# A graph layer on one core: a product padded to 128 rows, x + beta spread over two engines, and another order in the first and last steps

## The reference

```python
h = jnp.maximum(_layernorm(x), 0.0)
edge_input = concatenate([h[src], h[dst], edge_attr_32, node_vec[src], node_vec[dst]])
messages = silu(edge_input @ mW1 + mb1) @ mW2 + mb2
aggregated = segment_sum(messages, dst, 50000)
u = silu(concatenate([h, aggregated, node_vec]) @ uW1 + ub1)
out = x + _layernorm(h + u @ uW2 + ub2) * ln_gamma + ln_beta
```

## Time and profile before

| | |
|---|---|
| median of 3 runs (lowest, highest) | 649.43 us (648.74, 649.60) |
| span of the profiled execution | 645.0 us |
| median less that span | 4.4 us |
| busy: PE, DVE, ACT, POOL | 609.0, 594.8, 541.5, 400.7 us |
| TensorE clock granted, mean | 0.987 of full speed |

### The profile page before, as it was taken

The page is one execution under the profiler, slowest core; times in us unless marked ns, Lnnn a source line. Parts: engine busy times, 40 slices in busy tenths (PEclk is TensorE's granted clock), DMA queues, the critical chain, the costliest instruction groups (busy, mean ns, idle before and its releaser), DMA issues.

```text
span 645.0 us, 16065 instructions
## 1 busy us (share of the span) xinstructions
PE 609.0 (94%) x3716; PEld 451.9 (70%) x3764; DVE 594.8 (92%) x2050; ACT 541.5 (84%) x1181; POOL 400.7 (62%) x397
## 2 busy tenths in 40 slices
PE   2888999999999999999999999999999999999972
PEld 1346777776776786786786777777777777777762
DVE  4646899999999999999999999999999999999787
ACT  1578999989989989989989999999999899899730
POOL 6777667567567667667667766766676756761000
PEclk9998999999999999999999999999999999999987
DMA  5645567677677577677587577677676676674432
GB/s 149 200 127 135 145 211 216 165 214 216 165 215 218 171 212 211 170 215 217 163 214 216 169 217 205 173 215 203 178 227 186 179 229 183 201 203 125 134 86 102
DMA packets 92206, 119.02 MB, mean 185 GB/s; under 512 B 20250, under 2 KB 65749, under 8 KB 92168
## 3 DMA queue, kind: packets, MB, share of 16 engines
q1 hardware_dynamic: 64868, 44.03, 25.4%
q10 hardware_dynamic: 14756, 48.66, 20.9%
q0 software_dynamic: 12544, 25.92, 18.9%
HBM read 79.63 MB, written 38.70 MB: 183 GB/s over the span
## 4 chain that ended last, share of the span: by engine, by line
PE 87%; DVE 4%; issue 2%; ACT 2%; POOL 2%; DMA 2%; SPq 0%; POOLq 0%; DVEq 0%; ACTq 0%
PE ps_hid L594 13%; PE ps_upd L606 13%; PE ps_hid L591 12%; PE ps_e L551 8%; PE ps_e L521 8%; PE ps_t L562 7%; PE ps_t L539 6%; PE ps_e L517 6%; PE ps_e L518 6%; PE ps_upd L608 6%; POOL ends_in L456 2%; PE ps_f L529 1%; DVE y_out L894 1%; ACT ends_norm L668 1%; DVE centred L864 1%
## 5 line engine op out<-in xcount | busy, mean ns | idle before, releaser
L456 POOL DMA_INDIRECT ends_in<-in_rows,end_idx x392 | 399.6, 1019 | 182.0 <-issue 167.1
L668 ACT ACTIVATE ends_norm<-ends_in,minus,rstd 128x128 f32<-128x128 f32 x392 | 160.0, 482 | 1.9 <-DVE minus L1008 1.9
L668 ACT ACTIVATE x_norm<-x_in,minus,rstd 128x128 f32<-128x128 f32 x392 | 155.5, 482 | 0.0
L594 PEld LDWEIGHTS ps_hid<-match,msg_in 113*128 113x128 f32 x784 | 102.6, 191 | 47.6 <-issue 37.1
L894 DVE SCALAR_TENSOR_TENSOR y_out<-centred,rstd,x_beta 128x128 f32<-128x128 f32 x392 | 115.4, 338 | 0.2
L606 PE MATMUL ps_upd<-w_out,hidden_n 128*128 128x128 f32 x784 | 105.0, 277 | 2.7 <-DVE centred L864 2.5
L864 DVE SCALAR_TENSOR_TENSOR centred<-ps_upd,stats,gamma_row 128x128 f32<-128x128 f32 x392 | 106.5, 339 | 0.0
L594 PE MATMUL ps_hid<-match,msg_in 113*128 113x128 f32 x784 | 103.6, 275 | 0.0
L591 PE MATMUL ps_hid<-h_t,w_node 128*128 128x512 f32 x196 | 100.4, 593 | 0.0
L606 PEld LDWEIGHTS ps_upd<-w_out,hidden_n 128*128 128x128 f32 x784 | 96.4, 194 | 3.3 <-DVE centred L864 3.3
L766 ACT ACTIVATE hidden_n<-ps_hid,node_bias 128x512 f32<-128x512 f32 x98 | 66.7, 681 | 32.5 <-PE ps_hid L594 32.5
(11 more groups left out here) (81 smaller groups left out, 653.6 us busy)
## 6 DMA issues: line engine op xcount, KB each, us to landing
out<-y_out ACTq DMA_DIRECT2D x48, 512.0 KB
x_in<-in_x_steps ACTq DMA_DIRECT2D x44, 512.0 KB
msg_in<-msgs SPq DMA_DIRECT2D x392, 56.4 KB
msgs<-msg SPq DMA_DIRECT2D x49, 258.0 KB
ends_in<-in_rows,end_idx POOLq DMA_INDIRECT x392
feat_t<-in_attr SPq DMA_DIRECT2D x25, 128.0 KB, 3.3
x_in<-in_x_steps SPq DMA_DIRECT2D x5, 512.0 KB
feat_t<-coords SPq DMA_DIRECT2D x98, 2.0 KB
```

Source lines behind the costliest of these rows:

```text
L456: nc.gpsimd.indirect_dma_start(out=dst, out_offset=None, in_=rows, in_offset=bass.IndirectOffsetOnAxis(ap=end_idx[s.slot // 2][:, s.slot % ...
L594: last = nc.tensor.matmul(ps_hid[:, cols(j)], msg_in[k.half][0:WINDOW + 1, j, 0:H], match[k.half][0:WINDOW + 1, j, :], start=False, stop=j ...
L668: return nc.scalar.activation(dst, source, function, bias=minus[was][:, c:c + 1], scale=rstd[was][:, c:c + 1])
```

## The change

It has these parts:

- The product of the edge features takes 128 rows: w_feat and feat_t are 128 partitions high, and the 94 rows beyond the 34 are cleared by DVE once, at the start.
- x + beta: of the eight tiles of a step, two (POOL_TILES) are summed by POOL, one iteration later than DVE's own, behind its gathers and behind a wait for the match of the step before. DVE sums the other six in two pieces of three, one behind root_r, one behind rstd. The load of x_in and y_out wait for POOL's sums too (x_beta_begun). The first two steps (FIRST_NODES) stay with DVE alone.
- centred has two buffers.
- First iterations: DVE makes the x statistics and x + beta ahead of its wait for the gathers. In iteration 3 PE turns x ahead of the ends, into ps_upd (turns_first); ACT copies h_t ahead of ends_t. ACT's three early norms are left behind hidden_e in the first full iteration. `keep_busy` has two products fewer and writes ps_hid.
- Last iterations: DVE makes the update's statistics between the two matches, and y_out and x + beta behind the roots. ACT stores at the end of its body. For the last three node steps (N_APART; of the very last, its second half) ACT multiplies centred by rstd into y_out (scale_centred), and DVE only adds x_beta, four tiles in one instruction.

```diff
+FIRST_NODES = 2
+POOL_TILES = 2
+N_APART = 3
...
+    def turns_first(self):
+        return self.mode == WHOLE and isinstance(self.n, int) and self.n == NODE_LAG - 1
+    def late(self):
+        return bool(self.node(-1)) and not self.edge(0) and not self.node(4)
+    def scaled_apart(self):
+        done = self.node(-2)
+        if not done or not isinstance(done.n, int) or done.n < NODE_STEPS - N_APART:
+            return range(0)
+        return range(N_TILES // 2 if done.n == NODE_STEPS - 1 else 0, N_TILES)
...
-        w_src, w_dst, w_feat = sb("w_src", [P, H]), sb("w_dst", [P, H]), sb("w_feat", [FEAT, H])
+        w_src, w_dst, w_feat = sb("w_src", [P, H]), sb("w_dst", [P, H]), sb("w_feat", [P, H])
-        feat_t = [sb(f"feat_t{b}", [FEAT, 2, E_STEP]) for b in range(RING // 2)]
+        feat_t = [sb(f"feat_t{b}", [P, 2, E_STEP]) for b in range(RING // 2)]
...
 POOL, body
+                prev, near = it.node(-1), it.node(1)
+                if prev and near:
+                    wait_apart(pool, x_loaded[near.slot], 16 * (near.fills4 + 1), pool_passed)
+                    wait_apart(pool, out_ready, near.n - RING + 1, pool_passed)
...
+                    wait_apart(pool, match_ready, 2 * prev.n + 2, pool_passed)
+                    nc.gpsimd.tensor_tensor(x_beta[near.slot][:, 0:POOL_TILES, :], x_in[near.slot][:, 0:POOL_TILES, :],
+                                            beta_row[:, :, :].broadcast_to([P, POOL_TILES, H]), ALU.add).then_inc(x_beta_begun, 1)
...
 PE, body
-                        keep_busy((5, 2, 4)[it.n - BEFORE_FLAG])
+                        keep_busy((5, 2, 2)[it.n - BEFORE_FLAG])
...
 ACT, body
+                def scale_centred():
+                    tiles = it.scaled_apart()
...
+                    act.wait_ge(centred_ready, 2 * done.n + 2)
+                    act.wait_ge(rstd_ready, 2 * it.stats_before() - 1)
+                    act.wait_ge(stored[done.half], 16 * done.fills2)
+                    for j in tiles:
+                        last = nc.scalar.activation(y_out[done.half][:, j, :], centred[done.half][:, j, :], ACT.Copy,
+                                                    scale=rstd[was][:, 2 * E_TILES + N_TILES + j:2 * E_TILES + N_TILES + j + 1])
...
-                norm_ends(range(EARLY_TILES))
+                early = 0 if isinstance(k.n, int) and k.n == 0 else EARLY_TILES
+                if early:
+                    norm_ends(range(early))
...
-                    if half == 0:
+                    if half == 0 and not it.late():
                         store_nodes()
                 copy_ends()
                 load_nodes()
                 norm_nodes()
+                if it.late():
+                    store_nodes()
...
 DVE, body
+                    if j in apart:
+                        if j == apart.start:
+                            dve.wait_ge(scaled, done.n - (NODE_STEPS - N_APART) + 1)
+                        if j % HALF:
+                            return
+                        tiles = slice(j, j + HALF)
+                        last = V.tensor_tensor(y_out[done.half][:, tiles, :], y_out[done.half][:, tiles, :], x_beta[done.slot][:, tiles, :], ALU.add)
...
                 if late:
                     match_nodes(0)
-                    match_nodes(1)
-                    for j in range(N_TILES):
-                        finish(j)
                     for j in range(0, N_TILES, 2):
                         y_stat(j)
+                    match_nodes(1)
...
+                if not k:
+                    if ahead:
+                        wait(dve, rstd_ready, 2 * it.stats_before())
+                    for j in range(0, N_TILES, 2):
+                        x_stat(ahead, j, next_stats)
+                    add_beta(0)
+                    add_beta(1)
...
-                if not k:
-                    add_beta()
+                if k and not late:
+                    add_beta(0)
...
                 V.scalar_tensor_tensor(rstd[b][:, at], root_q[:, at], ROOT_B[1], root_r[:, at], ALU.add, ALU.mult).then_inc(rstd_ready, 1)
+                if k and not late:
+                    add_beta(1)
...
-                if k:
-                    add_beta()
...
+                if late:
+                    for j in range(N_TILES):
+                        finish(j)
+                    add_beta(0)
+                    add_beta(1)
```

More of the change, by code:

```diff
@@ L222, in gnn_layer @@
         hidden_n = sb("hidden_n", [P, N_STEP])
-        centred = sb("centred", [P, N_TILES, H])
+        centred = [sb(f"centred{b}", [P, N_TILES, H]) for b in range(2)]
         y_out = [sb(f"y_out{b}", [P, N_TILES, H]) for b in range(2)]
@@ L536, in turn_nodes @@
                     wait(pe, x_copied, near.n)
-                    wait(pe, ends_copied, edges_copied)
+                    if not it.turns_first():
+                        wait(pe, ends_copied, edges_copied)
+                    turned = ps_upd if it.turns_first() else ps_t
                     for j in range(N_TILES):
-                        last = nc.tensor.transpose(ps_t[:, cols(j)], x_norm[near.half][:, j, :], ident)
+                        last = nc.tensor.transpose(turned[:, cols(j)], x_norm[near.half][:, j, :], ident)
                     last.then_inc(x_transposed, 1)
@@ L691, in copy_nodes @@
                     wait(act, update_summed, 2 * near.n - 2)
-                    nc.scalar.activation(h_t[near.half][:, :], ps_t[:, :], ACT.Identity, bias=b2_col[:, :]).then_inc(x_copied, 1)
+                    turned = ps_upd if it.turns_first() else ps_t
+                    nc.scalar.activation(h_t[near.half][:, :], turned[:, :], ACT.Identity, bias=b2_col[:, :]).then_inc(x_copied, 1)
                 def evict_messages():
@@ L739, in norm_nodes @@
                     last.then_inc(x_norm_ready, 1)
+                scale_centred()
                 if not k:
@@ L760, in body @@
                 evict_messages()
-                norm_ends(range(EARLY_TILES, 2 * E_TILES))
+                norm_ends(range(early, 2 * E_TILES))
                 for half in range(2):
@@ L788, in _ @@
             V.memset(ones[:, SEARCH:], 1.0).then_inc(search_ops, 1)
+            for b in range(RING // 2):
+                V.memset(feat_t[b][:, :, :], 0.0).then_inc(feat_cleared, 1)
             dve.wait_ge(seen_loaded, 16)
@@ L899, in finish, with add_beta @@
                         last.then_inc(out_ready, 1)
-                def add_beta():
+                def add_beta(half):
                     if not later:
                         return
-                    if k:
-                        dve.wait_ge(x_loaded[later.slot], 16 * (later.fills4 + 1))
-                    wait(dve, out_ready, later.n - RING + 1)
-                    if isinstance(later.n, int) and later.n == 0:
-                        dve.wait_ge(late_loaded, 16 * N_LATE)
-                    V.tensor_tensor(x_beta[later.slot][:, :, :], x_in[later.slot][:, :, :],
-                                    beta_row[:, :, :].broadcast_to([P, N_TILES, H]), ALU.add).then_inc(x_beta_ready, 1)
+                    if half == 0:
+                        if k:
+                            dve.wait_ge(x_loaded[later.slot], 16 * (later.fills4 + 1))
+                        wait(dve, out_ready, later.n - RING + 1)
+                        if isinstance(later.n, int) and later.n == 0:
+                            dve.wait_ge(late_loaded, 16 * N_LATE)
+                    own = POOL_TILES if k else 0
+                    middle = (own + N_TILES) // 2
+                    tiles = slice(own, middle) if half == 0 else slice(middle, N_TILES)
+                    last = V.tensor_tensor(x_beta[later.slot][:, tiles, :], x_in[later.slot][:, tiles, :],
+                                           beta_row[:, :, :].broadcast_to([P, tiles.stop - tiles.start, H]), ALU.add)
+                    if half == 1:
+                        last.then_inc(x_beta_ready, 1)
                 def x_stat(n, j, into):
@@ L931, in y_stat @@
                         last.then_inc(y_stats, 1)
-                late = prev and not new and not ahead
+                late = it.late()
                 def between(j):
@@ L968, in body @@
                 if not (new or nxt or prev):
-                    for j in range(0, N_TILES, 2):
-                        x_stat(ahead, j, next_stats)
-                    add_beta()
                     return
@@ L1006, in body @@
                 V.scalar_tensor_tensor(rstd[b][:, at], root_q[:, at], ROOT_B[1], root_r[:, at], ALU.add, ALU.mult).then_inc(rstd_ready, 1)
+                if k and not late:
+                    add_beta(1)
                 dve.wait_ge(rstd_ready, 2 * it.stats_before() + 1)
                 V.scalar_tensor_tensor(minus[b][:, at], own_stats[:, at, MEAN], -1.0, rstd[b][:, at], ALU.mult, ALU.mult).then_inc(rstd_ready, 1)
-                if k:
-                    add_beta()
-                if not (k or late):
-                    for j in range(0, N_TILES, 2):
```

(3 more changed lines are left out.)

40 lines of the change are left out of this document (30 added, 10 removed).

## The result

The changed kernel is slower: 656.13 us median of 4 runs (654.81 to 657.83) against 649.15 for the kernel before on the same chip (648.74 to 649.60). The ratio is 1.0114, 95% interval 1.0096 to 1.0132. The forecast was 631.8, in a range of 628.5 to 640.0. The profiled execution took 656.15, with a span of 654.3 (645.0 before).

What follows compares the result with a forecast made beforehand. PE was taken as the bound at 12.006 us a step, DVE close behind. Gains of 13.1 (middle), 2.9 (start) and 2.8 (end) less 1.2 (ACT) made 17.6: span 627.4, time 631.8, range 628.5 to 640.

Steps and rivals of the forecast that it cites:

- the one on POOL: POOL's queue: the sum costs 0.95 a step, making 11.45, under PE's 11.71, and starts where the gathers end.
- Slower: Rival, chance 0.05: POOL's sum holds DVE's match each step; slower from a hold of 0.73, up to 665.8 us.
- the 4.4: Distance from the profiled span, 645.0, to the median time, 649.43, kept to turn span 627.4 into 631.8.
- another engine takes the bound: Rival, chance 0.25: DVE or POOL limits the middle steps, gaining only 0.1 to 0.2 a step; time 636 to 641.
- The row count: Feature product on PE: its 34-row form costs 0.29 us a step; rival that it is not the cause, 0.05.
- The worth of 13.1: Middle of the kernel: 0.29 us saved on PE in each of 45 steps, if nothing else becomes the bound.
- DVE at 11.40: DVE's step falls from 11.85 to 11.40: 0.21 less work in x + beta, 0.24 of waits hidden by the pieces.
- POOL's price: POOL's sum of 256 elements with its gap: 0.55 to 1.1 us a step, taken as 0.95.
- ACT's loss: ACT's hidden_e in the middle steps has little margin: 0 to 0.05 a step lost, 1.2 us in all.
- The first steps: Start of the kernel: reordered ACT, PE and DVE work gains 2.9 us, or 0 if the gathers take it back.
- The last steps: End of the kernel: y_stat between the matches and ACT's scaling gain 2.8 us, or 1.0 if scaling is late.

Runs made afterwards that it cites:

- the first experiment: The changed kernel without POOL's sum, DVE adding beta to all eight tiles in two pieces of four: 633.43 us, ratio 0.9733 to the kernel before.
- experiment 2: The kernel before with only the feature product widened to 128 rows, 94 of them zero: 645.16 us, ratio 0.9903.
- experiment 7: The changed kernel without POOL's sum, DVE doing all of x + beta in one piece behind minus: 638.37 us, ratio 0.9821 to the kernel before.
- experiment 3: The changed kernel with POOL's sum waiting for the match of its own iteration, so it lies in the centring: 647.53 us, ratio 0.9937 to the kernel before.

## Why the prediction was wrong

**The step that failed** is the one on POOL: "the sum will start where the gathers happen to end", with "DVE early in its step puts POOL's sum into the centring" as the reason to price the hold at nothing. The gathers don't happen to end anywhere. In every second step they start anew when the next indices land (the 3.43 of idle at 408.77; by the view of end_idx POOL waits 46.9 us for them, 20 times), and SP issues that DMA behind its eight windows, at a steady point of the step. Sixteen gathers and two sums take what they take, and so the sum comes to the same few places of DVE's step, and they are y_out, in 38 of 45. The trace of the kernel before had the place in it. POOL's eighth gather of two steps in a row, the one that starts anew between them, and then DVE:

```profile
400.26 0.94 POOL L456 DMA_INDIRECT ends_in<-in_rows,end_idx  x1 [0.30 <-issue]
403.76 0.95 POOL L456 DMA_INDIRECT ends_in<-in_rows,end_idx  x1 [2.55 <-issue]
413.50 1.02 POOL L456 DMA_INDIRECT ends_in<-in_rows,end_idx  x1 [0.30 <-issue]
```

```profile
401.11 0.59 DVE L894 SCALAR_TENSOR_TENSOR y_out<-centred,rstd,x_beta 128x128 f32<-128x128 f32 x2
414.48 1.40 DVE L880 SCALAR_TENSOR_TENSOR match<-iota_sb,const_sb,msg_in 112x512 f32<-112x512 f32 x2
```

The eighth gather ends at 401.20, among the y_out, and at 414.52, as the match begins. So it goes in all but three steps from 78 to 583 us; only in those three does it end in the centring. What is at a steady distance from another engine is not spread over its step, and the mean chance of a collision is no measure of it.

What happened is the case given 0.05, *Slower*, in its mechanism: a hold each step that DVE stands still for. Two details of it were off. It falls on y_out, not on match, and it is longer than the sum that causes it. Its threshold was right: a hold of 0.73 a step was to turn the sign; by the step, 12.33 - 11.40, it is 0.93 (0.86 of it in the group of y_out, the rest in the few matches and what I can't assign). The time is 7.0 above that of the kernel before on its chip; in the span, 45 x (12.33 - 12.006) less the gains of the ends, 14.6 - 5.3, is 9.3. The two differ by what is said below of the 4.4.

The second case, *another engine takes the bound*, had seen the place ("DVE reads two tiles from SBUF in y_out and match, POOL two in its sum") and priced it by "half its length each step, 0.5". The gather of 1.97 in the earlier trace rows was the warning: there the one that came second waited for about the whole of the other, not half. Taking the whole 0.73 to 0.95 for the term would have given DVE 12.1 to 12.35 and "no change or slower" as the forecast.

The Trainium skill, SBUF — State Buffer, Who interferes with whom, says that a DVE instruction with two SBUF inputs contends with a GpSimd instruction that reads SBUF, not with one that only writes it. The runs agree: 0.7 to 1.0 us of hold with the sum, 0.31 with a copy, none with a fill, none in the centring, which reads one tile from SBUF. That the blocked one waits for the whole of the other, as the same section has it, is not what the copy shows, 0.31 for 0.44.

**The row count** was the cause of the loss around the feature product, as predicted: 0.95 and 1.05 became 0.86, and the products and the turn behind them stand as the sum 0.86 + 0.86 + 0.11 had them. The worth of 13.1 was right for PE alone: most steps of the first experiment are 11.71. The mean is 11.84 there, since a few are longer, three of them by DVE's wait for late gathers.

**DVE at 11.40** was right: minus at 403.47 and at 415.88 in the changed kernel are 12.41 apart, with one hold of 1.01 between, so 11.40 without it. DVE's step of the kernel before was taken from one step, 11.85, and is about 11.96 in the mean (experiment 2). The pieces hid what they should; in experiment 7, with two pieces of four, 0.13 a step is left of it, since PE's 11.71 ends the gain.

**POOL's price** was right: 0.73 to 0.86 a sum, of 0.55 to 1.1 with its gap. It was the wrong thing to ask: whether POOL has the time, not whom it stops.

**ACT's loss** of 0 to 0.05 a step isn't there: with the fill the mean step is 11.79, and the 0.08 above PE's 11.71 is in five of the 45 steps (13.27, the first of them, 12.80, 12.33, 11.90 and 11.81; in the 12.80 and the 12.33 DVE had waited 1.12 and 1.07 for gathers). The others are 11.71, one 11.73.

**The first steps** were 2.9 by the sum and 2.97 by the second full product, by the mechanisms named, the late minus among them.

**The last steps** were mis-sized, 1.2 for 2.8. The scaling by ACT and the sums of DVE (1.29 for two) are as forecast, with the 0.76 of wait at 649.72 for the 0.9 that I had allowed. What is missing is ahead of them. The statistics were to fill the 1.35 of wait ahead of the second match; the wait now lies ahead of the first, 2.48, where nothing fills it. And that the new order puts a store of 512 KB beside the windows was in the diff, and I didn't cost it. In the first experiment the order is worth 2.3, and 0.9 of the rest comes back when the store is moved.

**The sum without the hold** looks right: the kernel with the fill runs at 631.9, and the forecast was 631.8. That is luck, two errors that cancel. Its span is 629.1, 1.7 above the forecast 627.4: the first full product 1.2 earlier than forecast, the 45 steps 2.1 longer, the last steps 0.8. And the 4.4 from span to time was no property of the kernel. The time of an execution is 1.8 to 1.9 above its own span (656.15 and 654.3 in the changed kernel, and the same in the other runs); the rest, 2.5, is that the profiled execution of the kernel before was shorter than its median.

**Open.** Why the hold of the sum, 1.01, is longer than its row, 0.73, isn't settled. The second y_out of the pair at 403.90 says where the surplus lies:

```profile
404.15 1.35 DVE L966 SCALAR_TENSOR_TENSOR y_out<-centred,rstd,x_beta 128x128 f32<-128x128 f32 x1
```

At its usual 0.34 it would have been over at 404.49, ahead of the sum's row (404.61 to 405.34), and it ends 0.16 behind that row. So the hold begins before the row and ends after it. What makes POOL pause for 1.9 every twelfth step is open too. That a POOL sum could be put into the centring without delaying POOL was not tried beyond experiment 3. The best versions are those without POOL's sum: 633.4, and with the store moved 632.1, 0.970 of the kernel before.

## What to carry to other kernels

Before work is given to an idle GpSimd, look at which DVE instructions read two operands from SBUF, and where in DVE's step the new instruction will lie; price a meeting at the whole length of it or more (the sum of 0.73 cost 0.69 to 1.03, the copy of 0.40 some 0.3), and every time, since engines coupled by waits meet at the same few places of the step; the trace of the kernel before shows where the queue of the idle engine ends. When DVE grows "busier" after a change, compare the longest instruction of each group with the shortest: a hold stands in no wait and in no median. And when a chain of DMAs ends a kernel, look for a large store beside it; moving one was worth 0.9 us of the tail by one trace each, which the medians don't tell from nothing.

## What the runs showed of the hardware

A GpSimd sum of 256 elements on 128 partitions (0.73 us alone) lengthened two DVE instructions of 0.34 us with two SBUF operands by 0.69 to 1.03; one of 128 elements by 0.24 and a match by 0.20; a copy of 256 (0.40 alone) by 0.31 in all; a fill of 256 (0.33) by nothing. The copy was held for 0.55 when a match had begun 0.03 ahead of it, so it goes both ways. A POOL sum beside one of DVE's two pieces of x + beta (two SBUF operands too) lengthened it from 0.56 to 1.09 (at 610.99 in the changed kernel). A fp32 product of 34 rows between products of 128 cost 0.29 us a step more than one padded to 128. A store of 512 KB issued among eight loads of windows went with a landing after 3.97 us, where the last of the eight took 1.85 in the kernel before, and in another kernel moving it took 1.1 off the wait for them.
